# Sums over edges taken two bodies behind their scores, seven passes of them in the scatter stage, in a graph attention layer

## The reference

```python
h = jnp.maximum(_layernorm(x, axis=-1), 0.0)
# node_features = h, edge_features = edge_attr_64, src, tgt = edge_index
h = node_features @ Wn + bn
q = node_features @ Wq + bq
k = node_features @ Wk + bk
v = node_features @ Wv + bv
eh = edge_features @ We + be
attn_in = jnp.concatenate([q[src], k[tgt], eh], axis=-1)
hmid = jax.nn.leaky_relu(attn_in @ A1 + b1, SLOPE)
scores = jax.nn.leaky_relu(hmid @ A2 + b2, SLOPE)
w = jax.nn.softmax(scores.mean(axis=-1), axis=0)
out = jax.ops.segment_sum(w[:, None] * v[tgt], src, num_segments=num_nodes)
y = h + out
# layer norm over the features with gamma and beta, and at the end: x + that
```

## Time and profile before

| | |
|---|---|
| median, lowest, highest of three runs | 6728.12, 6712.86, 6747.91 us |
| span of the profiled execution, first to last instruction | 5084.8 us |
| mean granted TensorE clock | 0.958 of full speed |
| busy: PE, DVE, POOL, ACT | 88, 78, 63, 55% of the span |
| DMA | 1276 MB, mean 251 GB/s |

### The profile page before, as it was taken

One profiled execution on the slowest core, in us unless ns is written; L12 is line 12 of the kernel. 1 busy time (PEld: TensorE's weight loads), 2 busy tenths in 40 slices (PEclk: granted clock), 3 DMA queues, 4 the chain that ended last, 5 costly groups with the idle time before them and its releaser, 6 DMA issues. The chain is left out here.

```text
span 5084.8 us, 136782 instructions
## 1 busy us (share of the span) xinstructions
PE 4453.7 (88%) x34924; PEld 3609.7 (71%) x35287; DVE 3986.4 (78%) x9657; ACT 2814.3 (55%) x7064; POOL 3197.2 (63%) x3381
## 2 busy tenths in 40 slices
PE   8655567888899999999999999999999987997887
PEld 3544455666688878888788878887888765777776
DVE  7655555777788888888888888888888774768998
ACT  5333333444466666666666666666666542446666
POOL 2677777777777777777777777777777772000110
PEclk9888888999999999999999999999999998999999
DMA  8888877888999988898888889988988765888888
GB/s 247 196 237 256 252 233 239 270 267 261 280 314 316 318 256 262 260 266 250 264 262 262 261 253 263 264 264 251 265 262 263 222 207 161 220 232 212 227 235 210
DMA packets 1938633, 1276.16 MB, mean 251 GB/s; under 512 B 637802, under 2 KB 1830929, under 8 KB 1938444
## 3 DMA queue, kind: packets, MB, share of 16 engines
q1 hardware_dynamic: 1768101, 831.59, 62.7%
q0 software_dynamic: 154752, 435.99, 23.1%
q10 hardware_dynamic: 15592, 6.41, 0.5%
HBM read 703.28 MB, written 570.23 MB: 250 GB/s over the span
## 5 line engine op out<-in xcount | busy, mean ns | idle before, releaser
L1272 POOL DMA_INDIRECT slots<-rows,slot_i x3224 | 3105.3, 963 | 992.2 <-issue 923.1
L1327 PE MATMUL ps_row<-win,mixed 128*128 128x256 f32 x5904 | 1535.6, 406 | 116.7 <-ACT rows L1419 114.9
L1327 PEld LDWEIGHTS ps_row<-win,mixed 128*128 128x128 f32 x5904 | 1119.0, 202 | 301.7 <-ACT rows L1419 134.4
L1419 ACT ACTIVATE rows<-ps_row 128x512 f32<-128x512 f32 x1476 | 889.5, 603 | 60.7 <-PE ps_row L1327 59.8
L1416 ACT ACTIVATE rows<-lo_all 128x8 f32 (+1 forms) x403 | 87.2, 216 | 1435.4 <-DMA slots<-rows,slot_i 1435.4
L1298 PE MATMUL ps_e<-ident,edges 128*128 128x128 f32 x3224 | 510.8, 283 | 263.1 <-ACT mixed L1408 171.3
L1298 PEld LDWEIGHTS ps_e<-ident,edges 128*128 128x128 f32 x3224 | 415.5, 146 | 427.4 <-ACT mixed L1408 181.1
L845 ACT ACTIVATE low<-ps_z 128x512 f32<-128x512 f32 (+1 forms) x882 | 528.2, 599 | 340.4 <-PE ps_z L774 160.5
L867 DVE TENSOR_TENSOR mid<-low,ps_z 128x512 f32<-128x512 f32 (+1 forms) x882 | 589.2, 668 | 125.9 <-ACT low L845 100.5
L774 PE MATMUL ps_z<-onehot,q_bits 128*128 128x512 bf16 (+1 forms) x2283 | 628.4, 376 | 19.5 <-DVE onehot L857 0.3
L1472 ACT ACTIVATE early_v<-early_v,early_weight 128x128 f32<-128x128 f32 x1960 | 600.0, 415 | 0.0
(11 more groups left out here) (217 smaller groups left out, 5716.5 us busy)
## 6 DMA issues: line engine op xcount, KB each, us to landing
u_rows<-slots SPq DMA_DIRECT2D x880, 258.0 KB, 3.2
early_v<-slots SPq DMA_DIRECT2D x490, 258.0 KB
edges<-edge_attr_dram SPq DMA_DIRECT2D x403, 256.0 KB
q_bits<-qb_tab SPq DMA_DIRECT2D x882, 96.0 KB, 3.0
slots<-no_row SPq DMA_DIRECT2D x98, 528.0 KB
slots<-rows,slot_i POOLq DMA_INDIRECT x3224
v_own<-slots SPq DMA_DIRECT2D x198, 258.0 KB, 3.4
slots<-no_row SPq DMA_DIRECT2D x98, 396.0 KB
```

What stands on the lines that cost most here:

```text
L1272: pool.indirect_dma_start(slots_tab[h], bass.IndirectOffsetOnAxis(slot_i[:, u, j:j + 1], 0), rows[:, u, j, :], None).then_inc(scattered[u] ...
L1327: last = pe.matmul(bank[:, j % 2, :], mixed[:, u % 2, j, :], win[:, u, :], start=True, stop=True)
L1419: nc.scalar.activation(rows[:, u, 2 * k:2 * k + 2, 0:2 * U0].rearrange("p j (a c) -> p j a c", a=2)[:, :, :, 0:D], row_bank(s, k).rearrang ...
```

## The change

Pairs are no longer summed pass by pass from body 14. The pairs of body n's eight units are summed in body n + 2 (`LAG` = 2), four in every body, from body 2 on, across the borders of the passes, and for seven passes in place of five. So there are 343 pairs in place of 245 in the scatter stage, and the last of them come behind the last step: `AFTER` is 16, the stage scores 686 units, and there are steps up to 419 that hold units (up to 410) and pairs, and no scatter.

The maximum is found for each body in place of each pass. DVE reduces the body's 32 scores, turns the result within groups of 32 partitions and reduces it again (`find_top`, at the end of the body's second step); PE spreads it with one small product (`spread_top`, in the third step), DVE reduces and takes the running maximum (`set_top`), ACT makes the weights of the body and two ratios (`raise_body`, at the end of the fourth).

In the sum stage two passes are left (`LATE` = 2). A block takes two steps in place of four; the last two parts of its finish and its store move one block back; `BLOCKS` is 8, so a loop body has the same 16 steps. The rows of x have four buffers (`XR` = 4). The scale of the sums so far is now one value for each body of the last early pass (`inv_of`).

```diff
-SOONER = 5
+SOONER = 7
+LAG = 2
 LATE = PASSES - SOONER
-SPOTS = 2 * LATE
+SPOTS = 8
-BLOCKS = 4
+BLOCKS = 8
+XR = 4
...
-        AFTER = 12
+        AFTER = 16
...
             def pair_begun(i, j):
 
-                n = i - SUM_BODY
-                if not 0 <= n < SUM_BODIES * SOONER:
-                    return None
-                q, r = n // SUM_BODIES, n % SUM_BODIES
-                return (q, r, j) if j < (PAIRS if r < SUM_BODIES - 1 else 1) else None
+                n = i - LAG
+                return ((n * PAIRS + j) // NQ, n, j) if 0 <= n * PAIRS + j < ALL_PAIRS else None
...
             def event_of(i):
-
-                n = i + 1 - SUM_BODY
-                return n // SUM_BODIES if n % SUM_BODIES == 0 and 0 <= n < SUM_BODIES * SOONER else None
+                return i - 1 if 0 < i <= LAST_BODY + 1 else None
...
+                    def spread_top(n):
+
+                        pe.wait_ge(top_made, n * 3 + 3)
+                        pe.matmul(ps_top, body_max[:, 0:1].to_broadcast([P, P]), ident[:, 0:P:32], start=True, stop=True,
+                                  skip_group_check=True).then_inc(top_sent, 1)
...
+                        sends = event is not None and u == 2
+                        if close is not None:
+                            bank_free(s + 1, *close)
+                        elif sends:
+                            pe.wait_ge(based, s + 1)
+                        if sends:
+                            spread_top(event)
+                        if close is not None:
+                            sum_early(*close)
+                        if more:
                             rank(s + 1, v)
...
+                    def raise_body(n):
+
+                        act.wait_ge(top_set, n * 2 + 4)
+                        nc.scalar.mul(body_max[:, 2:3], run_top[:, bass.ds(n + 1, 1)], -1.0 / H).then_inc(early_ready, 1)
+                        act.wait_ge(early_ready, n * 3 + 1)
+                        if not scaled[0]:
+                            act.sem_inc(early_ready, 1)
+                        else:
+                            nc.scalar.activation(ratio[:, bass.ds(n * 2, 2)], run_top[:, bass.ds(n - FIRST_RATIO, 2)], ACT.Exp,
+                                                 bias=body_max[:, 2:3], scale=1.0 / H).then_inc(early_ready, 1)
+                        w = units_left(o, n) * UNIT
+                        nc.scalar.activation(early_weight[:, 0:w], score[:, bass.ds(n * (BODY * UNIT), w)], ACT.Exp, bias=body_max[:, 2:3],
                                              scale=1.0 / H).then_inc(early_ready, 1)
...
+                    def find_top(n):
+
+                        dve.wait_ge(o.scored, n + 1)
+                        dve.sem_inc(passed, 1)
+                        w = units_left(o, n) * UNIT
+                        nc.vector.tensor_reduce(body_top[:, 0, 0:1], score[:, bass.ds(n * (BODY * UNIT), w)], AX_X, ALU.max).then_inc(top_made, 1)
+                        dve.wait_ge(top_made, n * 3 + 1)
+                        nc.vector.transpose(body_top[:, 1, :], body_top[:, 0, :]).then_inc(top_made, 1)
+                        dve.wait_ge(top_made, n * 3 + 2)
+                        nc.vector.tensor_reduce(body_max[:, 0:1], body_top[:, 1, :], AX_X, ALU.max).then_inc(top_made, 1)
...
-        BUNCHES = (1, 1, 2, 2)
+        BUNCHES = (1, 2)
...
                 def root(i, k):
 
-                    if k % LATE != 2 or not past(i, k - LATE):
+                    if k % LATE != 1 or not past(i, k - LATE):
...
                 def store(i, k, all_wide):
 
-                    if k % LATE == LATE - 1 and past(i, k - LATE):
-                        store_block(i * BLOCKS + (k // LATE - 1), (k // LATE - 1) % 2, all_wide)
+                    if k % LATE == 0 and past(i, k - 2 * LATE):
+                        store_block(i * BLOCKS + (k // LATE - 2), (k // LATE - 2) % 2, all_wide)
...
-                    if has(i, k) and past(i, k - LATE):
-                        for part_of in ((), (1, 2), (3,), (4, 5))[k % LATE]:
-                            finish(i * BLOCKS + (k // LATE - 1), (k // LATE - 1) % 2, part_of)
+                    if has(i, k):
+                        for back, part_of in (((2, 4), (2, 5), (1, 1), (1, 2)), ((1, 3),))[k % LATE]:
+                            if past(i, k - back * LATE):
+                                finish(i * BLOCKS + (k // LATE - back), (k // LATE - back) % 2, part_of)
```

397 lines of the change are left out of this document (212 added, 185 removed).

## The result

The changed kernel takes 6569.48 us (median of four runs, 6536.36 to 6596.5), the kernel before 6738.01 us in runs beside it (6712.86 to 6748.64). The ratio is 0.9753, with a 95% interval from 0.9714 to 0.9793: 168 us less, where 109 were forecast, and 20 us under the low end of the range.

A forecast was written before the change was run, and what follows sets the result against it. POOL's issues were taken to bound the scatter stage and DVE the sum stage; -157 + 0 + 0 + 55 - 7 = -109 us took 6728 to 6620 us, with 1643.3 us outside the span carried over; range 6590 to 6690.

The forecast's parts named there:

- Part 2: Scatter stage: 98 more pairs in the steps lie beside POOL's work and cost 0 us.
- the pace of the stage by POOL: Scatter stage: POOL's issues set the pace, 1.26 us each, 10.13 us for a step of eight.
- the cover of the added pairs: Scatter stage: added pairs stay hidden beside POOL; a 27 us slowdown from full DMA would just fit its 30-us lead.
- the first chance of the list: Chance 0.60 for the forecast's own case, a time of 6595 to 6650 us.
- Part 1, the sum stage: Sum stage: two of four passes go, a block falls from 4.934 to 3.31 us with DVE full, gain 157 us.
- The rival of a block of 3.9 us: Sum stage: 0.6 us lost in each block above its DVE work, gain only 100 there, 6676 us; chance 0.15.
- Part 3, the maximum: Scatter stage: a maximum for each body makes PE stand 0.95 us a body, within its spare 1.3 us; cost 0.
- both rivals of the wait: Scatter stage paced by PE's wait for the maximum: 2.2 us a body, 6681 us, chance 0.13; 3.5 us, 6789 us, 0.06.
- the lead of 30 us as cover: Scatter stage: the last fill's lead of some 30 us on POOL was counted as hiding delays up to that size.
- Part 4, behind the last step: Last fill to `ok_i`: eight steps of 8.2 us and nine of 5.0, 111 us, 55 more than before.
- The end of the range with the whole tail at 1.2 GHz: Behind the last step: PE wholly at its slow clock, 135 us, 80 more than before, 6645 us as the time.
- Part 5: Score stage: 196 units in place of 200, one batch of four less, 6.6 us gained.

The follow-up runs named there:

- experiment 4: Pair products cut to 2 of 8 in both kernels; where before takes 6767.27 us: before with the cut 6737.71, after with it 6580.53, after uncut 6732.49 us.
- after_fourth: The changed kernel, unchanged, on a chip where the kernel before takes 5077.64 us: 4963.47 us, ratio 0.9771.
- after_again: The changed kernel once more, unchanged, on a chip where the kernel before takes 6738.33 us: 6572.42 us, ratio 0.9756.
- before_more: The kernel before, unchanged, traced beside after_again: 6738.33 us.
- after_third: The changed kernel, unchanged, on a chip where the kernel before takes 6767.27 us: 6732.49 us, ratio 0.9944.

## Why the prediction was wrong, point by point

**What failed** is one step, the one that joined the trace to the times: "the median of the runs is 1643.3 us above it, and I carry that over unchanged". The page gave a span of 5084.8 us and no time of its own beside it; the times were 6728. I read the gap as something outside the first and last instruction. It was the difference between executions on two kinds of chip, and all of it lies in the steps: 14.1 to 14.6 us for a step in place of 10.1. The term of the sum that this made wrong is Part 2, the 0 for the steps, which rested on POOL as their pace: in the traces they are 45 us shorter. The forecast was -109 us; the traces give -166, and the 57 between them are -45 in the steps, -9 in the sum stage, -5 in the score stage, +2 in the tail and -1 at the end (rounded). With that, the pace of the stage by POOL, the cover of the added pairs and the first chance of the list were statements on an execution that the measured one was not. 1643 us outside a program of 5085 should have been a rival of its own, with its price: in a stage that POOL does not pace, everything added to PE, DVE or ACT may cost up to its own time, and the range would have had to be wider by tens of us on both sides.

**Part 1, the sum stage**: right, -165.4 and -165.7 us for -157. DVE's busy time for a block fell from 4.67 us (236.47 of 250) to 3.02 (225.15 of 240), 1.65 for the 1.62 counted, and the block by 1.70. The rival of a block of 3.9 us did not occur. But a cause that could have made it come true was not in the text: the whole gain of this stage hangs on XR = 4, which the prediction passes over. With two places the block is 6.0 us and the change a loss of 2%.

**Part 2, the pairs in the steps**: 0 forecast. Right on the 5080-us chips, where POOL's last issue moved by 1 us, less than its spread. On the first 6740-us chip the steps together are 45 us shorter, on the second some 80 longer by the estimate of experiment 4. So the term has no one value on these chips.

**Part 3, the maximum**: the three instructions took 0.18, 0.21 and 0.18 us (0.61 forecast), PE's wait was 1.1 us (0.75 forecast, 0.95 with the product). The waits didn't pace POOL on the 5080-us chips and hardly occurred on the others, so both rivals of the wait fell. The part that was off is the lead of 30 us as cover. The last fill stands 33.2 to 35.2 us ahead of POOL's last issue in three traces of the kernel before, 30.1 and 30.4 in two of the steps of after, and 16.5 and 17.8 with the added delay.

**Part 4, behind the last step**: 111 us forecast; 107.3, 105.9 and 108.7 measured. The end of the range with the whole tail at 1.2 GHz, 135 us, did not occur: in after_fourth the granted clock was 1.00 in 4204 to 4262 us and 0.84 in 4230 to 4330, again between the levels. The eight steps with units took 7.6 us each, from the last fill at 4217.2 to 4278.10, for the 8.2 taken. The steps with a pair alone took 5.0 us each, the value chosen between 4.0 and 5.8. The first two and the last two of the nine products of a pair alone (PE, after_fourth; the first and the last are eight steps apart):

```profile
4278.10 3.53 PE L1378 MATMUL ps_rank<-early_v,early_spot 128*128 128x128 f32 x16 [1.00 <-issue]
4283.51 2.70 PE L1378 MATMUL ps_rank<-early_v,early_spot 128*128 128x128 f32 x16 [1.89 <-DVE acc_sb L1684]
...
4313.96 2.45 PE L1378 MATMUL ps_rank<-early_v,early_spot 128*128 128x128 f32 x16 [1.89 <-DVE acc_sb L1684]
4318.30 3.75 PE L1378 MATMUL ps_rank<-early_v,early_spot 128*128 128x128 f32 x16 [1.89 <-DVE acc_sb L1684]
```

(4318.30 - 4278.10)/8 = 5.03 us, of which 1.89 are idle on PE: DVE makes the next one-hots only when the products have read the last, and adds the sum behind them (1.29 and 0.47 us), before the next products start.

**Part 5**, the score stage: -9.2 and -11.6 us for -7.

**The sum** on the chips for which the trace of before stood: -114 us measured (ratio 0.9771) for -109. Where the result was measured: -168; in the traces -166, of which -121 are these terms and -45 the steps. On the first kind no term is off by more than 9 us, and the errors partly cancel, so the near hit is mostly the terms and in small part luck.

**What stays open**: why ACT and DVE start late behind PE's products on some chips, and why nearly only at the higher clock; and why, with that, the steps of the changed kernel are shorter by 45 us on one 6740-us chip and longer by some 80 on another. In 2000 to 5700 us PE is idle for 0.27 us a step less in after_again than in before_more. The part that ends on nothing recorded is larger (2.1 us a step for 1.9); the part ended by DVE is smaller (0.6 for 1.0), and in after_third, on the second chip, it is 1.2. That describes the difference and is no cause. On the second chip there is no trace of before itself.

## What to carry to other kernels

Set the span of a profile against the time of the same execution before a term is added to either; if the gap is more than a few us, the profile may be of another pace than the times, and each term that rests on "covered by the bound engine" needs its price for the case that this engine is not the bound.

A change that shortens a loop's body also shortens the time in which its buffers come round: for each queue ask which wait stands ahead of the loads that the shorter body needs, and how many bodies lie between taking a place and freeing it. Here two more places of 128 by 128 were worth 270 us in their stage, 288 in all.

A lead of a producer over the bound engine covers delays only if what follows starts on the bound engine; if it starts on the producer, every us that the lead loses is paid at the border.

## What the runs showed of the hardware

The same program takes 5078 to 5082 us on two chips and 6738 to 6767 on two others, with single instructions of ACT and POOL as long (`rows` 600 to 603 ns at the median, the sends 960 to 963), loads that land as fast (3.2 us for `u_rows`) and the stages behind the steps equal within 10 us. In the steps the granted TensorE clock is 0.88 on the second two (before_more) and 1.00 on the first two.

On the chips of the second kind ACT starts up to 9.3 us behind the end of PE's record, on those of the first 0.04 us, 0.12 at most; from ACT to DVE it is 0.03 us on both. Of the waits over 2 us in after_again 94 followed a product at 2.4 GHz and 2 one at 1.2 GHz.

A transposition of 128x32 f32 in squares of 32 took 0.21 us on DVE. One-hots of 128x128 f32 (TENSOR_SCALAR) took 0.41 us on the mean and up to 0.62 beside POOL's additions in SBUF, and 0.35 at most without them.
